# Layer normalisation of a ViT tower on Trainium2: one more centred buffer, centring by halves, statistics on four 32-wide tiles

## The reference, cut to what matters

```python
def _layernorm(x, axis=-1, eps=1e-05):
    m = jnp.mean(x, axis=axis, keepdims=True)
    v = jnp.var(x, axis=axis, keepdims=True)
    return (x - m) / jnp.sqrt(v + eps)

h = _L0_tok_ref(x, ...)
h = h + _L0_attn_ref(_layernorm(h, axis=-1), ...)
h = h + _L0_ffn_ref(_layernorm(h, axis=-1), ...)
h = h + _L1_attn_ref(_layernorm(h, axis=-1), ...)
h = h + _L1_ffn_ref(_layernorm(h, axis=-1), ...)
```

## Time and profile before

| | us |
|---|---|
| median of 3 runs | 2259.73 (2258.05 to 2263.02) |
| the profiled execution, its own time | 2260.83 |
| its span in the trace | 2258.8 |
| TensorE busy | 2060.8 (91%) |
| VectorE busy | 1163.8 (52%) |
| ScalarE busy | 1019.3 (45%) |
| GpSimd busy | 617.2 (27%) |

### The profile page before, as it was taken

How to read it: one execution, slowest core, us unless ns; L and a number is a source line. 1 busy time by engine, 2 the same in 40 slices (tenths; PEclk the granted TensorE clock), 3 DMA queues, 4 the chain that set the end, 5 groups by cost and what they waited for, 6 DMA issues and landing times. The chain is left out here.

```text
span 2258.8 us, 69505 instructions
## 1 busy us (share of the span) xinstructions
PE 2060.8 (91%) x27135; PEld 1570.6 (70%) x27135; DVE 1163.8 (52%) x3589; ACT 1019.3 (45%) x3029; POOL 617.2 (27%) x853
## 2 busy tenths in 40 slices
PE   6999987999899997767997999999978999999999
PEld 2444445667676666466554787878847999999999
DVE  0000036778777775497224555555535555555555
ACT  0000035565555553412444555555535555565555
POOL 0000004778777775000000343333410000000000
PEclk9999999999999999855998999999988999999999
DMA  7776600000000000200000000000000000000000
GB/s 304 290 305 263 251 1 2 3 3 3 3 3 3 3 3 3 83 1 0 0 0 1 2 3 2 2 2 2 3 1 5 9 8 7 8 8 8 8 7 10
DMA packets 22322, 91.74 MB, mean 41 GB/s; under 512 B 5092, under 2 KB 13548, under 8 KB 15596
## 3 DMA queue, kind: packets, MB, share of 16 engines
q1 hardware_dynamic: 20302, 86.00, 9.7%
q10 hardware_dynamic: 1822, 2.68, 0.3%
HBM read 84.41 MB, written 4.26 MB: 39 GB/s over the span
## 5 line engine op out<-in xcount | busy, mean ns | idle before, releaser
L1402 ACT ACTIVATE hidden_m<-ps,s_f_b 128x128 f32<-128x128 f32 x1040 | 297.2, 369 | 225.7 <-PE ps L1345 222.4
L812 PE MATMUL ps<-xn,s_a_wqkv 128*128 128x260 f32 x1024 | 288.7, 405 | 13.8 <-ACT qk_a L558 8.4
L1345 PE MATMUL ps<-xn,s_f_w 128*128 (+1 forms) x2080 | 287.5, 282 | 0.4 <-ACT hidden_m L1402 0.4
L153 PE MATMUL ps<-x_chunk,s_w_tok 128*128 128x512 f32 x576 | 252.9, 598 | 21.6 <-DMA s_cls<-in_cls 21.6
L1481 DVE SCALAR_TENSOR_TENSOR acc_m<-ps,weights_m,acc_m 128x128 f32<-128x128 f32 x520 | 182.5, 351 | 153.6 <-ACT acc_m L1425 105.1
L1345 PEld LDWEIGHTS ps<-xn,s_f_w 128*128 128x128 f32 x2080 | 255.1, 193 | 8.4 <-ACT hidden_m L1402 0.7
L1357 PE MATMUL ps<-s_f_w,hidden_m 128*128 128x128 f32 x2080 | 253.6, 275 | 0.0
L1357 PEld LDWEIGHTS ps<-s_f_w,hidden_m 128*128 128x128 f32 x2080 | 242.6, 192 | 1.6
L153 PEld LDWEIGHTS ps<-x_chunk,s_w_tok 128*128 128x128 f32 x576 | 108.8, 191 | 163.9 <-issue 142.3
L812 PEld LDWEIGHTS ps<-xn,s_a_wqkv 128*128 128x128 f32 x1024 | 175.9, 192 | 57.6 <-ACT qk_a L558 20.3
L1331 POOL COPY xn_tile_m<-xn 128x128 f32 (+1 forms) x65 | 19.1, 294 | 550.2 <-PE ps L1384 494.1
(11 more groups left out here) (199 smaller groups left out, 4234.2 us busy)
## 6 DMA issues: line engine op xcount, KB each, us to landing
x_chunk<-in_x_main SPq DMA_DIRECT2D x48, 1536.0 KB, 9.4
out<-acc_m SPq DMA_DIRECT2D x65, 64.0 KB, 1.5
s_f_w<-in_f_w SPq DMA_DIRECT2D x2, 1024.0 KB
x_chunk<-in_x_tail SPq DMA_DIRECT2D x16, 96.0 KB, 12.5
s_w_tok<-in_w_tok ACTq DMA_DIRECT2D x1, 1216.0 KB, 9.6
s_a_wqkv<-in_a_wqkv ACTq DMA_DIRECT2D x1, 768.0 KB
s_a_wqkv<-in_a_wqkv SPq DMA_DIRECT2D x1, 768.0 KB
s_f_w<-in_f_w SPq DMA_DIRECT2D x2, 256.0 KB
```

The costliest lines, as they stand in the source:

```text
L153: nc.tensor.matmul(ps[:, a.slot, :], w_tok[:, k, :], xb[:, a.slot, k, :], start=(k == 0), stop=False)
L812: nc.tensor.matmul(ps[:, QK_BANK[i], 0:QUAD], w_qkv[:, c * P:(c + 1) * P], xn[:, t.h * QUAD:(t.h + 1) * QUAD], start=True, stop=True).then ...
L1345: last = nc.tensor.matmul(ps[:, b % 2, i * P:i * P + n], w1[:, c * P:(c + 1) * P], xn[:, bass.ds(a.index * n, n)], start=True, stop=True)
L1402: last = nc.scalar.activation(hid[:, a.slot, c, :], ps[:, b % 2, i * P:i * P + n], ACT.Relu, bias=b1[:, c:c + 1])
```

## The change

`mean_w` takes the place of `pick_mean`, and `spread_w`, 1/32 everywhere, that of `pick_spread`. The centred halves go through three banks (0 to 2), each with its own copy and its own signal; the square reads `xc` in SBUF, which has four buffers, and waits for ScalarE's own copies; the variance uses one bank (3) and four column tiles of 32; the spread uses four row tiles of 32 rows and one bank for each quarter (4 to 7); `normalise` is one product of 832 columns.

```diff
-    QP = P // 2
+    QP = P // Q
+    SX = 4
-        xc = sb(f"centered_{tag}", [P, 3, 2, half])
-        sq = sb(f"squared_{tag}", [P, 2, 2, half])
+        xc = sb(f"centered_{tag}", [P, SX, Q, n])
+        sq = sb(f"squared_{tag}", [P, 2, Q, n])
...
             def center(g):
-                since(pe, copied, g - 1)
-                since(pe, squared, g - 1)
-                for k in range(2):
-                    last = nc.tensor.matmul(ps[:, g % 2 * 2 + k, 0:half], center_w[:, :], columns(h, g, k),
-                                            start=True, stop=True)
-                last.then_inc(center_ps, 1)
+                for q in (2 * g, 2 * g + 1):
+                    since(pe, copied, q - 2)
+                    nc.tensor.matmul(ps[:, q % 3, 0:half], center_w[:, :], h[:, q * half:(q + 1) * half],
+                                     start=True, stop=True).then_inc(center_ps, 1)
 
             def variance(g):
                 pe.wait_ge(squared, g + 1)
-                since(pe, sd_done, g - 1)
-                for b in range(2):
-                    for a in range(2):
-                        last = nc.tensor.matmul(ps[a * QP:(a + 1) * QP, 4 + g % 2, 0:n], pick_mean[:, b, :],
-                                                sq[:, g % 2, a, b * n:(b + 1) * n], start=(b == 0), stop=(b == 1))
+                since(pe, sd_done, g)
+                for i in range(Q):
+                    last = nc.tensor.matmul(ps[i * QP:(i + 1) * QP, 3, 0:n], mean_w[:, 0:QP],
+                                            sq[:, g % 2, i, :], start=True, stop=True)
                 last.then_inc(var_ps, 1)
 
             def spread(g):
                 pe.wait_ge(rstd_done, g + 1)
-                since(pe, normed, 2 * g)
-                for b in range(2):
-                    for a in range(2):
-                        rows = slice(a * QP, (a + 1) * QP)
-                        last = nc.tensor.matmul(ps[:, 6 + a, b * n:(b + 1) * n], pick_spread[rows, b, :],
-                                                rstd[rows, g % 2, :], start=True, stop=True)
-                        if b:
-                            last.then_inc(spread_ps, 1)
+                since(pe, normed, g)
+                for i in range(Q):
+                    rows = slice(i * QP, (i + 1) * QP)
+                    last = nc.tensor.matmul(ps[:, 4 + i, 0:n], spread_w[rows, :], rstd[rows, g % 2, :],
+                                            start=True, stop=True)
+                last.then_inc(spread_ps, 1)
...
-                nc.scalar.activation(sd[:, g % 2, :], ps[:, 4 + g % 2, 0:n], ACT.Sqrt, bias=eps[:, 0:1])\
+                nc.scalar.activation(sd[:, g % 2, :], ps[:, 3, 0:n], ACT.Sqrt, bias=eps[:, 0:1])\
...
-                    act.wait_ge(center_ps, g + 1)
-                    since(act, normed, 2 * g - 4)
-                    two = slice(g % 2 * 2, g % 2 * 2 + 2)
-                    nc.scalar.activation(xc[:, g % 3, :, :], ps[:, two, 0:half], ACT.Copy).then_inc(copied, 1)
+                    since(act, normed, g - SX + 1)
+                    for q in (2 * g, 2 * g + 1):
+                        act.wait_ge(center_ps, q + 1)
+                        nc.scalar.activation(xc[:, g % SX, 2 * (q % 2):2 * (q % 2) + 2, :],
+                                             ps[:, q % 3, 0:half].rearrange("p (i n) -> p i n", n=n),
+                                             ACT.Copy).then_inc(copied, 1)
+                    act.wait_ge(copied, 2 * g + 2)
                     since(act, var_ps, g - 1)
-                    nc.scalar.activation(sq[:, g % 2, :, :], ps[:, two, 0:half], ACT.Square).then_inc(squared, 1)
+                    nc.scalar.activation(sq[:, g % 2], xc[:, g % SX], ACT.Square).then_inc(squared, 1)
...
-                since(dve, spread_ps, 2 * g - 2)
+                since(dve, spread_ps, g - 1)
...
             def normalise(g):
-                dve.wait_ge(copied, g + 1)
-                for k in range(2):
-                    dve.wait_ge(spread_ps, 2 * g + k + 1)
-                    nc.vector.tensor_tensor(columns(xn, g, k), xc[:, g % 3, k, :], ps[:, 6 + k, 0:half],
-                                            ALU.mult).then_inc(normed, 1)
+                dve.wait_ge(copied, 2 * g + 2)
+                dve.wait_ge(spread_ps, g + 1)
+                nc.vector.tensor_tensor(xn[:, g * Q * n:(g + 1) * Q * n].rearrange("p (i n) -> p i n", n=n),
+                                        xc[:, g % SX], ps[:, 4:4 + Q, 0:n], ALU.mult).then_inc(normed, 1)
...
 fold_first:
             nc.vector.memset(mean_w[:, :], 1.0 / D).then_inc(folded, 1)
-            nc.vector.memset(pick_mean[:, :, :], 0.0).then_inc(folded, 1)
-            nc.vector.memset(pick_spread[:, :, :], 0.0).then_inc(folded, 1)
-            dve.wait_ge(folded, 3)
-            for b in range(2):
-                nc.vector.memset(pick_mean[:, b, b * 32:(b + 1) * 32], 1.0 / D).then_inc(folded, 1)
-                for a in range(2):
-                    nc.vector.memset(pick_spread[a * 64 + b * 32:a * 64 + (b + 1) * 32, b, :], 1.0 / 32)\
-                        .then_inc(folded, 1)
+            nc.vector.memset(spread_w[:, :], 1.0 / 32).then_inc(folded, 1)
```

More of the change, by code:

```diff
@@ L178, in _, with layer_norm @@
             pipelined(dve, chunks, 2, 0, 2, step)
-def layer_norm(nc, tag, tokens, h, xn, ps, center_w, pick_mean, pick_spread, loads=()):
+def layer_norm(nc, tag, tokens, h, xn, ps, center_w, mean_w, spread_w, loads=()):
     n = 208
     Q = 4
-    QP = P // 2
+    QP = P // Q
     half = 2 * n
@@ L208, in layer_norm @@
         block = ctx.enter_context(nc.Block())
-        def columns(t, g, k):
-            return t[:, g * Q * n + k * half:g * Q * n + (k + 1) * half]
         def since(eng, sm, value):
@@ L1488, in fold_first @@
 def fold_first(nc, ps, mean_w, ident, w_v, alpha_col_raw, alphas, bv_col, w_out, b_out, b_out_all, b_q, neg_b_q,
-               w_cls, dist_pair, pick_mean, pick_spread, center_w):
+               w_cls, dist_pair, spread_w, center_w):
     ctx, sb, sem = stage_scope(nc)
@@ L1551, in _ @@
             nc.vector.tensor_copy(w_cls[:, :], ps[:, 3, 0:D]).then_inc(folded, 1)
-            dve.wait_ge(folded, 14)
+            dve.wait_ge(folded, 7)
 def fold_second(nc, ps, ident, w_v, w_out, w_cls, wt_t, w_out2, w_dist):
@@ L1612, in vit_tower @@
         center_w = ctx.enter_context(nc.sbuf_tensor("center_w", [P, P], FP32))
-        pick_mean = ctx.enter_context(nc.sbuf_tensor("pick_mean", [P, 2, 64], FP32))
-        pick_spread = ctx.enter_context(nc.sbuf_tensor("pick_spread", [P, 2, D], FP32))
+        spread_w = ctx.enter_context(nc.sbuf_tensor("spread_w", [P, P], FP32))
         alphas_raw = ctx.enter_context(nc.sbuf_tensor("alphas_raw", [SEQ, ORDER, H], FP32))
@@ L1640, in vit_tower @@
                    alphas, S["a0_bv"][:, :], S["a0_wout"], S["a0_bout"][:, :], b_out0, S["a0_bqk"][:, 0:CH],
-                   neg_b_q, w_cls, dist_pair, pick_mean, pick_spread, center_w)
-        layer_norm(nc, "a0", tokens, h, xn, ps, center_w, pick_mean, pick_spread)
+                   neg_b_q, w_cls, dist_pair, spread_w, center_w)
+        layer_norm(nc, "a0", tokens, h, xn, ps, center_w, mean_w, spread_w)
         attention(nc, "a0", images, h, xn, ps, S["ident"], S["a0_wqkv"], S["a0_wout"], S["a0_wout_sw"], b_out0,
@@ L1649, in vit_tower @@
         w_dist = ctx.enter_context(nc.sbuf_tensor("w_dist", [P, D], FP32))
-        layer_norm(nc, "f0", tokens, h, xn, ps, center_w, pick_mean, pick_spread, rest)
+        layer_norm(nc, "f0", tokens, h, xn, ps, center_w, mean_w, spread_w, rest)
         with nc.sbuf_tensor("gate_all", [P, tokens], FP32) as gate_all:
@@ L1656, in vit_tower @@
                     S["a1_wt_t"], S["a1_wout2"], w_dist)
-        layer_norm(nc, "a1", tokens, h, xn, ps, center_w, pick_mean, pick_spread)
+        layer_norm(nc, "a1", tokens, h, xn, ps, center_w, mean_w, spread_w)
         attention(nc, "a1", images, h, xn, ps, S["ident"], S["a1_wqkv"], S["a1_wout"], S["a1_wout_sw"],
                   S["a1_bout"], None, None, w_cls, None, w_dist, S["dist"], dist_pair, mean_w)
-        layer_norm(nc, "f1", tokens, h, xn, ps, center_w, pick_mean, pick_spread)
+        layer_norm(nc, "f1", tokens, h, xn, ps, center_w, mean_w, spread_w)
         dense_mixture(nc, tokens, h, xn, ps, S["ident"], S["f1_gate"], S["f1_gate_b"], S["expert_ids"],
```

## The result

The changed kernel took 2218.24 us (median of 4 runs, 2216.84 to 2220.25), the kernel before, beside it, 2258.89 (2254.39 to 2263.02). The ratio is 0.9821, with a 95% interval from 0.980 to 0.9842. The forecast was 2222, with a range from 2213 to 2234. The profiled execution took 2218.98 us, its span 2217.1, which is 41.7 less than the span of before.

What follows compares the result with a forecast made beforehand. A chain of waits through three centred buffers was taken to bound the normalisations. Intervals 32.2, fill and drain 4.4 and weights 0.7 sum to 37.3 us saved, giving 2222 us, range 2213 to 2234.

Steps and rivals of the forecast that it cites:

- The old ring: Normalisations before: with three centred buffers, the copy of group g waits for normalise of g-3, 4.46 us a group.
- The new ring: Normalisations after: waits from centring through copy, square, reciprocal, products and spread close once in two groups, 6.62 us, 3.31 each.
- The square from SBUF: ScalarE's square reading SBUF instead of PSUM: 0.90 us where it took 0.857, about 0.6 us in all.
- Four row tiles abreast: Spread on TensorE: four 32-row tiles run at once, two waves instead of four, 0.55 us instead of 0.90.
- two abreast: Rival: row tiles run two at a time, spread stays 0.90, 3.49 us a group, near 2230; chance 0.17 with similar misses.
- Costs put at nothing: Normalisations: one variance bank's later wait is hidden, and three centring banks by halves cost nothing.
- Weights: In fold_first nine memsets become two, so the reduction of the alphas starts earlier: 0.7 us saved.
- Fill and drain: Start and end of each normalisation stage: 0.5 and 0.6 us saved, together 1.1 a stage, 4.4 in all.
- Looser ring: Rival: hand-overs too long or halves slip forward, so TensorE's own 2.65 us a group is the floor, 2204; chance 0.07.
- lower clock: Rival: TensorE at 1.2 GHz throughout, its load 5.0 us a group, 14 us more, near 2274; chance 0.03.
- no change in the middle: Rival: a misread wait keeps the per-group limit; only fill, drain and weights gain, 2256; chance 0.04.

Runs made afterwards that it cites:

- kernel 1: Kernel before the change with a fourth centred buffer and nothing else: 2228.49 us, ratio 0.9857.
- kernel 2: Changed kernel with three centred buffers instead of four, all else kept: 2255.52 us, ratio 0.998.
- kernel 5: Changed kernel with VectorE doing the products of group g-1 ahead of the reciprocal of g: 2220.77 us, ratio 0.9837.
- kernel 3: Changed kernel with the spread on two row tiles of 64 rows, as before the change: 2228.30 us, ratio 0.9857.
- kernel 6: Changed kernel with TensorE issuing the spread one group later (g-3 instead of g-2): 2198.34 us, ratio 0.9734.
- (4): Changed kernel with the variance on two column tiles of 64, still in one bank: 2217.09 us, ratio 0.9813.

## Why the prediction was right, and where not

**The old ring.** Right. The third buffer's wait set the pace: with it alone lifted the interval falls to 3.56 (1), with it alone put back it is 4.57 (2).

**The new ring.** Right, with its place and its size. I had summed 6.62 us for two groups; the rows make it 6.54, and 23.12 us over seven intervals, four long and three short, are 3.30 where I said 3.31. That the two agree to 0.01 is partly luck: my terms were 0.04 a group too long, and I had not counted that of seven intervals in turn longer and shorter four are long, which adds 0.03. By term: the copy 0.516 for 0.52; the wait for ScalarE's own copies 0.02 for 0.05; the square 0.896 and its step 0.81, for 0.90 and 0.79; deviation to reciprocal 0.45 for 0.47; products and hand-over to the spread 1.10 for 1.17, since one product of 832 takes 0.96 there and not 1.02; spread 0.57 for 0.55. The order on VectorE (5), the spread's length (3) and the spread's place on TensorE (6) each moved the pace; the variance's length (4) did not.

**The square from SBUF.** 0.857 has become 0.896, the 0.04 that was taken from the exponential's fixed part. The square now reads SBUF where it read PSUM, and nothing else of its shape changed. So the trace agrees in direction with what the Trainium skill, page "VectorE: DVE Perf Modes", section Specifications, says of ScalarE's place near PSUM. The prediction says that no size is given; that holds for this section, but further down the same page of the Trainium skill, in the section "The TRN2 errata — SBUF-src ops pay a fixed extra latency per instruction", a table gives ScalarE 224 fixed cycles from SBUF and 172 from PSUM. At the table's 1.2 GHz that is an estimate of 0.043 us, and the traces have 0.039. By the ring the 0.04 costs 0.02 a group, and only as long as the square is on it; no kernel here ran the square from PSUM with the other edits in place.

**Four row tiles abreast.** Right: eight records in 0.63 us, the next mode 0.57 after the first. The rival of two abreast would have shown 0.97, as kernel 3 does. That agrees with the fourfold tiling that the page "TensorEngine Tiling (Array Packing)" of the Trainium skill gives for a contraction of 32 (section Theoretical Speedup). Two waves of 208 columns take 0.35 of the 0.57 by the prediction's 0.175 a record; the rows do not tell what the other 0.2 goes into, loading weights, changing the mode or both.

**Costs put at nothing.** The single variance bank was hidden: in 40 groups the variance waited four times for the deviation that frees its bank, 2.0 us in all, each time in the last group of a stage, as in this row of the changed kernel. The deviation behind it ended at 332.85, long before the reciprocal that reads it started (333.94):

```profile
331.80 0.56 PE L236 MATMUL ps<-squared_a,mean_w 128*32 128x208 f32 x8 [0.49 <-ACT deviation_a L265]
```

The three banks by halves were free: TensorE waited 0.7 us in all for a copy, three times (the line of the copies, L273, who waited for it).

**Weights.** Right: from the first record of `fold_first` to that of the normalisation it was 7.24 us and is 6.58. Both ran at the lower clock there (the same eight records took 1.84 and 1.87 us), so the two can be compared.

**Fill and drain.** Here a term was mis-sized. I put 1.1 us a stage, 4.4 in all; it was 2.2 for the fill, where I had 2.0, and 4.4 for the drain where I kept 0.6 a stage, 2.4 in all. The third stage, filled at the full clock in both traces, bears out the 0.5 a stage (9.28 to 8.77 us). I had read the drain in the first stage alone, where before only the last spread was slow. In the third and fourth stage both of the last two were (the kernel before, the third stage):

```profile
1222.63 1.73 PE L251 MATMUL ps<-rstd_a,pick_spread 64*128 64x208 f32 x8 [1.92 <-DVE xn L300]
...
1225.63 1.76 PE L251 MATMUL ps<-rstd_a,pick_spread 64*128 64x208 f32 x8 [1.27 <-DVE xn L300]
```

The stages' tails of before were 6.1, 6.4, 7.1 and 7.1 us long; now each is 5.57. The last two spreads of the four stages took 12.2 us together before and 7.0 now. Not all of this is owed to the narrow tiles: kernel 1 has the old ones, ran three of its four drains at the higher clock and had 3.5 us of the 4.4. How much of the drain's gain is tiles and how much the clock that a stage's end happens to be granted, one trace of each kernel cannot divide.

**The rest.** 39.0 in the stages and 0.7 in the fold leave 2.0 of 41.7. The first attention, whose code is the same, was 3.0 us shorter, and the patch embedding 1.3 longer. Over the ten traced kernels that attention took between 552.7 and 556.6 us, in no order with their edits, but in step with the granted clock (columns as in the earlier trace rows; before, then changed):

```profile
348.12:904.70 556.58, 494.45 (x12930) 377.87 (x12930) 412.48 (x1216) 311.22 (x867) 412.16 (x449) 0.98 0.01 3
...
338.91:892.45 553.54, 490.90 (x12930) 375.04 (x12930) 412.64 (x1216) 311.01 (x867) 412.16 (x449) 0.99 0.01 3
```

In microseconds at the lower level that is 17.3 before and 7.4 now. The four traces in which the attention took 554.1 or less had 6.9 to 9.9 of them, the six in which it took 555.2 or more had 12.6 to 20.5. So this part goes with the clock, and no run shows that the change set it. Another 0.4 us does go with the change and was not in the sum: from the last record of `fold_second` to the first of the third normalisation it is 0.90 us in the three kernels with the old tiles and 0.49 in the seven with the new code; no run shows why. My point was 3.8 us above the median; some half of this is the drain and half the rest described here.

**The rivals.** Looser ring, lower clock and no change in the middle are out; between the first products and the eighth every stage was granted 1.00. So it was before: the 0.98 of the earlier trace rows comes from the window's first 1.5 us, in the fill (304.5 to 342: 1.00). The looser ring's price, TensorE's own 2.65, was right as a number: kernel 6 runs at it.

## What to carry to other kernels

When a pipeline over several engines is slower than each of them, write down each wait as a ring, with the number of groups after which it closes, and divide its length by that number. One more buffer lifts one ring and the next longest decides; price that one before you expect more, and look whether a step issued one group later lengthens the ring's span of groups, which needed no memory here and gave half of the change's gain again. Judge a narrower tile or a cheaper copy only once the ring that hides it is open. And read fill and drain in every stage, with the granted clock beside them, before an edit gets the credit for them.

## What the runs showed of the hardware

Products of 832 columns that had to wait for the spread took 1.02 us (all 40 in kernel 5, four of 40 in the changed kernel), and 0.96 where they ran right behind the reciprocal (the other 36), on the same operands.

The same eight records of `fold_first` (L1512) took 1.87 us in the changed kernel's trace and 1.05 in that of kernel 2, in which nothing is changed there; the stage was 1.4 us shorter with it. The windows around them (columns as in the earlier trace rows) show the granted clock at its lower level, 1.2 GHz, in the changed kernel's trace:

```profile
294.80:297.00 2.20, 2.12 (x10) 2.12 (x11) 0.78 (x3) 0.00 (x0) 0.00 (x0) 0.50 0.00 0
```

and at 2.4 GHz in that of kernel 2:

```profile
294.10:295.50 1.40, 1.31 (x11) 1.31 (x12) 0.80 (x3) 0.00 (x0) 0.00 (x0) 1.00 0.00 0
```

What TensorE had done before was the same patch embedding in both. The level at which it enters a short stage is worth more here than the edit of the weights, and differs between executions.
